# A nucleus search in a graph kernel: one full vector evaluation fewer and one aimed point more in step one

## Chip, cores and metric
The kernel runs on one core of a Trainium2 chip. The metric is the device time of one execution in microseconds, all float32. Engines are named as in the profile: PE (TensorE matmul), PEld (its weight loads), DVE (VectorE), ACT (ScalarE), POOL (GpSimd) and SP (SyncE, which issues the DMAs).

## What is computed
Four graph layers run over x (3327 rows of 256) and a sparse weighted 3327 x 3327 adjacency. The third layer is where the change sits. For each of its two steps every row of a dense attention matrix is cut to its nucleus, the largest entries that together hold 90% of the row:

```
n, D_ATTN, STEPS, P_NUC = 3327, 64, 2, 0.9
def _adj_from_feats(Xa, W1, W2, W3):
    logits = (Xa @ W1) @ W2 @ (Xa @ W3).T
    idx  = argsort(-logits, axis=1)
    csum = cumsum(softmax(sorted logits), axis=1)
    k_i  = sum(csum < P_NUC, axis=1) + 1
    keep the k_i largest of each row; return softmax(kept logits)
for s in range(STEPS):
    A  = _adj_from_feats(Xa, W1, W2, W3)
    Xf = Rf @ Xf;  Xb = Rb @ Xb;  Xa = A @ Xa
    Z  = Z + Xf @ U1[s] + Xb @ U2[s] + Xa @ U3[s]
Y = X + Z, then a layer norm, scaled and shifted
```

## The kernel before
The 3327 rows are padded to 26 tiles of 128 rows (NT = 26). Layers 0 and 1, layer 3 and the two attention steps are written as software pipelines. The attention part is one loop of `rounds`. In each round one tile is at each stage, and each engine runs its own written-out order. Steps one and two follow each other in the same loop: tiles 0 to 25 are step one, tiles 26 to 51 step two, with LAG = 5 rounds between them.

In a round, PE computes the scores of a tile L in four pieces (L910), the transposes of the finished tile T (L895), the product of its probabilities with the values (L882), the neighbour sums for another tile (L922) and small dense products (L929, L954, L958). ACT copies each of these out of PSUM: L1070 the scores into `E`, L1066 the transposes into `PT`, and others. PE can't go on to the next piece before ACT has copied. ACT also takes the exponential of tile F (L1075) and runs the passes of the aimed search (L1027). Every such pass reads the full tile of 128 x 3327.

The sorted nucleus isn't computed by sorting. A threshold for each row is searched in three parts:

- POOL makes a first guess of the threshold from the row's mean and sum (`guess`, L1204 to L1236).
- ACT evaluates an aimed point: a pass with `Relu` sums what lies above it (m = 0), a pass with `Sign` counts it (m = 1). `PASSES` is 2 for each point and `POINTS` is 2. POOL then corrects the threshold from the two sums (`update(t, j)`, L1238 to L1276), with a Newton-like step for the first point and a secant-like one for the second. Each point narrows a bracket `ends2`. The corrections work on columns of 128 x 1 to 128 x 4 elements, and `then` makes POOL wait for each group before it issues the next.
- DVE evaluates the threshold exactly (`find`, L1367 on) `EVALS` times: 3 in step one and 4 in step two. Each evaluation is one SCALAR_TENSOR_TENSOR over 128 x 3327 (L1399) with short instructions around it. Then L1406 collects what lies below the upper end, and a loop takes the eight largest remaining entries with MAX8 (L1420) and MATCH_REPLACE8 (L1430). The loop runs again if a row of the tile still needs more. L1446 writes the kept probabilities.

DVE's order in a round is the row maximum of tile F (L1361) and then `find` of tile S. The tiles stand two rounds apart: F = shown(i - 1), R = shown(i - 2), S = shown(i - 3), T = shown(i - 4).

POOL's order in a step-one round is: guess(F), update(R, 1), the two adds of the neighbour sums of tile G (L1328, L1332), update(F, 0). The second point of a tile is thus corrected one round after its first. In step two the adds and layer norm pieces of further tiles stand around these (L1296 to L1347).

ACT's order: piece 0 ends with the exponential of F and then sums(R, 1, 0). Piece 1 ends with sums(R, 1, 1), piece 2 with sums(F, 0, 0). Piece 3 has sums(F, 0, 1) right after the copy of the last scores. `aimed[j]` tells ACT that point j is there, `summed[j]` tells POOL that a pass is done, `bracketed` tells DVE that the aimed search has ended.

Of the kernel before, what the change touches and what calls it, by code (L numbers as in the profile page):

```python
# [13 lines left out]
P = 128  # L14
# [18 lines left out]
UNDER = 1.0 - 2.0 ** -22  # L33
# [41 lines left out]
def build(nc, n_nodes, xin, adjT, W0T, b0, W1g, A1T, A2, A3, UA, UB, UC, gamma, beta, tin, Wg3, out):  # L75
# [13 lines left out]
    with ctx:  # L89
# [551 lines left out]
        with ExitStack() as att:  # L641
# [11 lines left out]
            sign = ab("sign", [P, 2, POINTS])  # L653
            negp = ab("negp", [P, 2, POINTS])
            known = ab("known", [P, 8])
            outset = ab("outset", [P, 2, 2, 2])
            ga = ab("ga", [P, 2, 20])
            up = ab("up", [P, 2, 24])
            cand = ab("cand", [P, 2, 3])
# [49 lines left out]
            kept = len(spread)  # L709
            turned = lambda i: sum(first(sent_at(k)) or first(post_at(k)) for k in range(i))  # L710
# [3 lines left out]
            with phase_semaphores(nc, "att_") as s:  # L714
# [30 lines left out]
                summed = [s(f"summed{j}") for j in range(POINTS)]  # L745
                aimed = [s(f"aimed{j}") for j in range(POINTS)]
                step_done, bracketed = s("aim_step"), s("bracketed")

                with nc.Block() as block:
# [264 lines left out]
                    def _(act):  # L1014
                        go = nc.scalar.activation

                        def sums(t, j, m):
                            if m == 0:
                                act.wait_ge(aimed[j], t + 1)
                                if j > 0:  # L1020
                                    act.wait_ge(summed[j - 1], PASSES[j - 1] * (t + 1))
                                elif t >= 1:
                                    act.wait_ge(summed[1], 2 * t)
                            else:
                                act.wait_ge(summed[j], 2 * t + 1)
                            func, acc_ = ((ACT.Relu, over), (ACT.Sign, sign))[m]
                            go(junk[:, 0:N], E[:, t % DEPTH, 0:N], func, bias=negp[:, t % 2, j:j + 1], scale=1.0,  # L1027
                               accum_out=acc_[:, t % 2, j:j + 1]).then_inc(summed[j], 1)

                        for i in range(rounds):  # L1030
# [11 lines left out]
                            for k in range(SLOTS):  # L1042
# [38 lines left out]
                                if k == 0 and R is not None:  # L1081
                                    sums(R, 1, 0)
# [84 lines left out]
                    def _(pool):  # L1167
# [3 lines left out]
                        KNOWN = (1.0 / ROOT, -1.0, 0.5, float(np.e), AIM[0], STEER[0], AIM[1], STEER[1])  # L1171
# [21 lines left out]
                        def offer(t, j):  # L1193
                            then(ts(negp[:, t % 2, j:j + 1], cand[:, t % 2, 0:1], -UNDER, None, ALU.mult))
                            pool.sem_inc(aimed[j], 1)

                        def prepare(t):
                            q, step = t % 2, t // NT
                            p = cand[:, q, 0:1]
                            then(ts(up[:, q, 0:2], known[:, 4 + 2 * step:6 + 2 * step], p, ga[:, q, 12:13], ALU.mult, ALU.add),  # L1200
                                 ts(up[:, q, 3:4], p, p, RIDGE[step] ** 2, ALU.mult, ALU.mult))
                            then(tt(up[:, q, 4:5], up[:, q, 3:4], ga[:, q, 11:12], ALU.mult))

                        def guess(t):  # L1204
# [5 lines left out]
                            p = cand[:, q, 0:1]  # L1210
                            pool.wait_ge(exp_done, t + 1)
                            if t >= DEPTH:
# [14 lines left out]
                            offer(t, 0)  # L1227
# [7 lines left out]
                                 ts(ga_(11), ga_(15), ga_(9), 1.0 / DENSITY, ALU.mult, ALU.mult))  # L1235
                            prepare(t)  # L1236

                        def update(t, j):  # L1238
                            q, d, step = t % 2, t % DEPTH, t // NT
                            up_ = lambda a: up[:, q, a:a + 1]  # L1240
                            restart()
                            p, gap_p, slip = (cand[:, q, a:a + 1] for a in range(3))
                            slope = ga[:, q, 11:12]
                            ends = ends2[:, d]
                            lo, hi = ends2[:, d, 0, 0:1], ends2[:, d, 1, 0:1]
                            tgt, point = trial2[:, d, GOAL:GOAL + 1], trial2[:, d, POINT:POINT + 1]
                            count, mass_ = up_(5 + j), up_(8 + j)
                            pool.wait_ge(summed[j], PASSES[j] * (t + 1))
                            then(ts(count, sign[:, q, j:j + 1], 0.5, N / 2, ALU.mult, ALU.add))
                            then(ts(mass_, count, p, over[:, q, j:j + 1], ALU.mult, ALU.add))  # L1250
                            then(ts(cand[:, q, 1:3], up[:, q, 0:2], mass_, None, ALU.add),
                                 ts(took[:, 1:2], mass_, tgt, None, ALU.is_ge))
                            if j > 0:
                                then(tt(up_(16), mass_, up_(7 + j), ALU.subtract))
                                then(ts(up_(17), up_(16), up_(16), up_(3), ALU.mult, ALU.add),
                                     tt(up_(18), up_(16), up_(20), ALU.mult))
                                then(tt(up_(19), up_(17), minus, ALU.pow),
                                     tt(up_(18), up_(4), up_(18), ALU.subtract))
                                then(tt(slope, up_(18), up_(19), ALU.mult))
                            then(tt(up_(21), slip, slope, ALU.mult),  # L1260
                                 ts(took[:, 0:3:2], took[:, 1:2].to_broadcast([P, 2]), -1.0, 1.0, ALU.mult, ALU.add))
                            wide = lambda ap: ap.unsqueeze(2).to_broadcast([P, 2, 2])
                            then(ts(up_(20), up_(21), STRIDE, -STRIDE, ALU.min, ALU.max),
                                 tt(parts[:, 0], ends, wide(took[:, 0:2]), ALU.mult),
                                 tt(parts[:, 1], cand[:, q, 0:2].unsqueeze(1).to_broadcast([P, 2, 2]),
                                    wide(took[:, 1:3]), ALU.mult))
                            then(tt(up_(22), e_, up_(20), ALU.pow),
                                 tt(ends, parts[:, 0], parts[:, 1], ALU.add))
                            then(tt(up_(23), up_(22), p, ALU.mult))
                            if j < POINTS - 1:  # L1270
                                then(ts(p, up_(23), hi, lo, ALU.min, ALU.max))
                                offer(t, j + 1)
                                prepare(t)
                            else:
                                then(ts(point, up_(23), hi, lo, ALU.min, ALU.max))
                                pool.sem_inc(bracketed, 1)  # L1276

# [10 lines left out]
                        for i in range(rounds):  # L1288
# [37 lines left out]
                            if first(G):  # L1326
# [166 lines left out]
```

## Time and profile before

| | us |
|---|---|
| median of 3 runs | 3486.06 (3485.86 to 3487.74) |
| the profiled execution | 3488.64 |
| its span in the profile | 3486.8 |
| PE, DVE, POOL, ACT busy | 3144.3, 2454.0, 2146.4, 1599.1 |

The span is from the first to the last instruction. Row maxima of step one (L1361) start from 818.56 to 1759.36 us, those of step two from 1899.43 to 3090.95 us. The page's first part gives the busy shares, 90% for PE, 70% for DVE, 62% for POOL and 46% for ACT. They are means over all layers. The chain that ended last is 6% of the span on PE's L294 in the last layer, and it says nothing about the attention stage.

### The profile page before, as it was taken

How to read it: one execution, taken by the hardware profiler on the slowest of the kernel's cores; microseconds unless marked ns; L12 is line 12 of the kernel's file. 1: busy time of each engine (PE TensorE's matmuls, PEld its weight loads, DVE VectorE, ACT ScalarE, POOL GpSimd, SP SyncE). 2: the span in 40 equal slices, each digit the busy share in tenths (PEclk: the TensorE clock that was granted, in tenths of full speed). 3: DMA queues.
4: the chain of work that ended last, by engine and by line, in shares of the span. 5: the costliest groups of instructions: out<-in, count | busy, mean ns of one | idle time of the engine just before them, and what ended most of it. 6: DMA issues, size and time to landing. Idle time of an engine off the chain costs nothing. (4 is left out here: it accounts for less than half of the span.)

```text
span 3486.8 us, 42119 instructions
## 1 busy us (share of the span) xinstructions
PE 3144.3 (90%) x13212; PEld 2272.6 (65%) x13212; DVE 2454.0 (70%) x3451; ACT 1599.1 (46%) x2357; POOL 2146.4 (62%) x4214
## 2 busy tenths in 40 slices
PE   4999989998699999999976698988899999996899
PEld 3788878885477777777754254544566566664788
DVE  6983410002998889888884799999978999998000
ACT  2211321225566666666653455555555655552200
POOL 1212421124788888888880677877988788886211
PEclk9999999998899999999988899999999999998899
DMA  6643444443122122112211111211222222223254
GB/s 246 223 162 132 130 147 163 163 142 86 44 58 58 58 58 66 54 59 63 65 33 62 47 52 52 62 44 56 57 81 76 73 84 82 74 83 102 91 201 172
DMA packets 140702, 327.59 MB, mean 94 GB/s; under 512 B 15456, under 2 KB 93664, under 8 KB 129248
## 3 DMA queue, kind: packets, MB, share of 16 engines
q1 hardware_dynamic: 140512, 325.30, 29.3%
q8 instruction: 90, 1.47, 0.2%
q14 instruction: 100, 0.82, 0.1%
HBM read 286.70 MB, written 38.54 MB: 93 GB/s over the span
## 5 line engine op out<-in xcount | busy, mean ns | idle before, releaser
L1027 ACT ACTIVATE junk<-E,negp 128x3327 uint8<-128x3327 f32 x208 | 637.3, 3064 | 142.4 <-issue 107.8
L1399 DVE SCALAR_TENSOR_TENSOR U<-E,trial 128x3327 f32<-128x3327 f32 x182 | 678.5, 3728 | 0.0
L922 PE MATMUL bank<-big,adj 128*128 128x512 f32 x1352 | 609.9, 602 | 8.7 <-ACT t L1053 8.7
L922 PEld LDWEIGHTS bank<-big,adj 128*128 128x128 f32 x1352 | 252.9, 192 | 329.2 <-issue 328.1
L294 PE MATMUL bank<-big,E 128*128 128x256 f32 x1664 | 366.2, 381 | 2.4 <-PEq L58 1.7
L882 PE MATMUL bank<-Hc,PT 128*128 128x256 f32 x1248 | 305.1, 396 | 69.2 <-ACT PT L1066 69.2
L294 PEld LDWEIGHTS bank<-big,E 128*128 128x128 f32 x1664 | 315.9, 191 | 49.3 <-issue 6.6
L882 PE MATMUL bank<-Hc,adj 128*128 128x256 f32 x1456 | 335.4, 382 | 10.7 <-ACT adj L1066 10.7
L1361 DVE TENSOR_REDUCE nmax<-E 128x1 f32<-128x3327 f32 x52 | 188.0, 3615 | 207.4 <-ACT E L1070 207.4
L882 PEld LDWEIGHTS bank<-Hc,PT 128*128 128x128 f32 x1248 | 245.9, 199 | 129.9 <-ACT PT L1066 79.7
L882 PEld LDWEIGHTS bank<-Hc,adj 128*128 128x128 f32 x1456 | 277.8, 191 | 72.9 <-issue 23.0
L922 PE MATMUL bank<-Hc,adj 128*128 128x256 f32 x1352 | 314.2, 383 | 1.0 <-ACT bias L1047 1.0
L922 PEld LDWEIGHTS bank<-Hc,adj 128*128 128x128 f32 x1352 | 253.6, 191 | 78.7 <-issue 48.6
L895 PE MATMUL tr<-ident,E 128*128 128x128 f32 x1352 | 192.4, 283 | 119.9 <-DVE E L1446 119.8
L1420 DVE MAX8 top<-U 128x8 f32<-128x3327 f32 x74 | 268.4, 3627 | 21.8 <-DVE mass L1408 11.9
L352 POOL TENSOR_TENSOR xn<-xt,t 128x256 f32<-128x256 f32 x52 | 37.7, 724 | 386.9 <-ACT t L325 205.8
L1430 DVE MATCH_REPLACE8 U<-mark,U 128x3336 f32<-128x3336 f32 x74 | 267.7, 3618 | 0.0
L895 PEld LDWEIGHTS tr<-ident,E 128*128 128x128 f32 x1352 | 168.4, 147 | 145.7 <-DVE E L1446 125.5
L910 PE MATMUL lg<-K,qt 64*128 64x384 f32 (+1 forms) x832 | 215.4, 596 | 33.1 <-ACT E L1070 25.2
L366 DVE TENSOR_TENSOR t<-bank,big 128x256 f32<-128x256 f32 x26 | 11.0, 425 | 286.9 <-PE bank L294 286.9
L1066 ACT ACTIVATE adj<-tr 128x1024 f32<-128x1024 f32 x104 | 95.4, 918 | 251.1 <-PE tr L895 251.1
L1070 ACT ACTIVATE E<-lg 128x1024 f32<-128x1024 f32 x208 | 179.4, 863 | 54.1 <-PE lg L910 48.7
(248 smaller groups left out, 5937.2 us busy)
## 6 DMA issues: line engine op xcount, KB each, us to landing
adj<-adjT SPq DMA_DIRECT2D x131, 448.0 KB, 3.4
E<-adjT SPq DMA_DIRECT2D x32, 1664.0 KB, 6.9
adj<-adjT SPq DMA_DIRECT2D x104, 384.0 KB, 3.4
adj<-adjT SPq DMA_DIRECT2D x20, 1664.0 KB, 7.0
E<-adjT SPq DMA_DIRECT2D x26, 1216.0 KB, 5.7
xt<-xin SPq DMA_DIRECT2D x52, 128.0 KB, 5.7
x_d<-xn SPq DMA_DIRECT2D x52, 128.0 KB, 1.7
xt<-x_d SPq DMA_DIRECT2D x52, 128.0 KB, 5.2
```

The costliest lines, as they stand in the source:

```text
L294: last = nc.tensor.matmul(acc[par][:, 0:D], bufs[par][:, j], rhs[:, j], start=(j == j0), stop=(j == NT - 1))
L882: last = mm(axp[:, 0:D], PT[k % 2][:, h, i * P:(i + 1) * P], Hc[:, j], start=(k == 0 and h == 0 and i == 0), stop=(k == SLOTS - 1 and h == ...
L895: last = nc.tensor.transpose(tr[:, h, i * P:(i + 1) * P], E[:, t % DEPTH, c0:c0 + P], ident[:])
L910: last = mm(lg[:, h, 0:w], qt[rows, t % 2], K2[rows, c0:c0 + w], start=True, stop=True)
L922: last = mm(agg[:, 0:w], adj[:, SPAN * (k % 2) + j - AGG[k]], rhs[:, j], start=(j == 0), stop=False)
L1027: go(junk[:, 0:N], E[:, t % DEPTH, 0:N], func, bias=negp[:, t % 2, j:j + 1], scale=1.0, accum_out=acc_[:, t % 2, j:j + 1]).then_inc(summed ...
L1066: go(PT[k % 2][:, :, 0:w], tr[:, :, 0:w], ACT.Copy).then_inc(pt_copied, 1)
L1070: go(halves(E[:, L % DEPTH])[:, :, c0:c0 + w], lg[:, :, 0:w], ACT.Copy, accum_out=musum[:, L % 2, k:k + 1]).then_inc(lg_copied, 1)
L1361: V_.tensor_reduce(nmax[:, t % DEPTH:t % DEPTH + 1], E[:, t % DEPTH, 0:N], axis=AX_X, op=ALU.max, negate=True).then_inc(max_ready, 1)
L1399: V_.scalar_tensor_tensor(out=U[:, 0:N], in0=e, scalar=point, in1=e, op0=ALU.is_ge, op1=ALU.mult, accum_out=found))
L1420: rthen(V_.memset(U[:, N:NPAD], 0.0), V_.max(top8[:], U[:, 0:N]))
L1430: V_.match_replace(U[:], mark[:], U[:], MARKED).then_inc(rnd, 1)
```

## The change
Step one gets three aimed points instead of two (`POINTS = (3, 2)`), and two exact evaluations instead of three. Step two keeps two points and four evaluations. The third point has a `Sign` pass only. The constants of the search change too. `summed` becomes one semaphore that counts ACT's passes in ACT's order.

ACT runs sums(R, 1, 0) at the end of piece 1, just ahead of sums(R, 1, 1), and no longer in piece 0. In step one sums(R, 2, 1) stands in piece 2, ahead of sums(F, 0, 0). POOL gets update(R, 2) in step one between the adds of tile G and update(F, 0).

`update` is rewritten. The first point goes from the counted pass to the next `negp` in five dependent steps, the second in eight. The new `negp` is the old one times the correction factor, without the clamp to the bracket. The bracket and the preparation of the next point come after `aimed` has been raised.

```diff
-EVALS = (3, 4)
+EVALS = (2, 4)
-PASSES = (2, 2)
-POINTS = 2
-SHIFT = (1.4, 0.0)
-STEER = (2.0, 4.0)
-AIM = (3.0, 4.0)
-KEEP_END = (0.8, 0.75)
+POINTS = (3, 2)
+SHIFT = (1.2, 0.0)
+AIM = (2.0, 4.0)
+KEEP_END = (0.8, 0.85)
-UNDER = 1.0 - 2.0 ** -22
+UNDER = 1.0 - 2.0 ** -20
...
                                 if k == 0 and R is not None:
-                                    sums(R, 1, 0)
...
                                     if R is not None:
+                                        sums(R, 1, 0)
                                         sums(R, 1, 1)
...
+                                    if R is not None and POINTS[R // NT] > 2:
+                                        sums(R, 2, 1)
                                     if F is not None:
                                         sums(F, 0, 0)
...
                         def prepare(t):
-                            p = cand[:, q, 0:1]
-                            then(ts(up[:, q, 0:2], known[:, 4 + 2 * step:6 + 2 * step], p, ga[:, q, 12:13], ALU.mult, ALU.add),
-                                 ts(up[:, q, 3:4], p, p, RIDGE[step] ** 2, ALU.mult, ALU.mult))
-                            then(tt(up[:, q, 4:5], up[:, q, 3:4], ga[:, q, 11:12], ALU.mult))
+                            up_ = lambda a: up[:, q, a:a + 1]
+                            p = up_(24)
+                            then(ts(up_(2), p, N / 2 + AIM[step], ga[:, q, 12:13], ALU.mult, ALU.add),
+                                 ts(up[:, q, 0:2], known[:, 4 + 2 * step:6 + 2 * step], p, None, ALU.mult),
+                                 ts(up_(3), p, p, RIDGE[step] ** 2, ALU.mult, ALU.mult))
+                            then(tt(up_(4), up_(3), ga[:, q, 11:12], ALU.mult))
...
                         def guess(t):
+                            then(ts(cand[:, q, 0:1], p, 1.0, None, ALU.mult))
                             prepare(t)
...
                         def update(t, j):
+                            if j < 2:
+                                pool.wait_ge(summed, nth[t, j, 0])
+                                then(tt(up_(5), over[:, q, j:j + 1], up_(2), ALU.add))
+                            pool.wait_ge(summed, nth[t, j, 1])
+                            if j < 2:
+                                then(ts(slip, signs, up_(0), up_(5), ALU.mult, ALU.add))
+                            else:
+                                then(ts(slip, signs, up_(16), up_(17), ALU.mult, ALU.add))
+                            if j == 0:
+                                then(ts(up_(13), slip, slope, STRIDE, ALU.mult, ALU.min))
+                            else:
+                                then(tt(up_(7), slip, up_(6), ALU.subtract))
+                                then(ts(up_(8), up_(7), up_(7), up_(3), ALU.mult, ALU.add),
+                                     ts(up_(9), up_(7), up_(10), up_(4), ALU.mult, ALU.add))
+                                then(tt(up_(11), up_(8), minus, ALU.pow),
+                                     tt(up_(12), up_(9), slip, ALU.mult))
+                                then(ts(up_(13), up_(12), up_(11), STRIDE, ALU.mult, ALU.min))
+                            then(ts(up_(14), up_(13), -STRIDE, None, ALU.max))
+                            then(tt(up_(15), e_, up_(14), ALU.pow))
+                            if not last:
+                                then(tt(negp[:, q, j + 1:j + 2], negp[:, q, j:j + 1], up_(15), ALU.mult))
+                                pool.sem_inc(aimed[j + 1], 1)
+                            if j < 2:
+                                then(ts(took[:, 1:2], slip, up_(1), None, ALU.is_ge),
+                                     tt(up_(21), up_(15), p, ALU.mult))
+                            else:
+                                then(ts(up_(18), signs, up_(19), up_(20), ALU.mult, ALU.add),
+                                     tt(up_(21), up_(15), p, ALU.mult))
+                                then(ts(took[:, 1:2], up_(18), 0.0, None, ALU.is_ge))
+                            then(ts(took[:, 0:3:2], took[:, 1:2].to_broadcast([P, 2]), -1.0, 1.0, ALU.mult, ALU.add))
+                            then(tt(parts[:, 0], ends, wide(took[:, 0:2]), ALU.mult),
+                                 tt(parts[:, 1], cand[:, q].unsqueeze(1).to_broadcast([P, 2, 2]),
...
+                            then(tt(ends, parts[:, 0], parts[:, 1], ALU.add))
+                            if last:
+                                then(ts(point, up_(21), hi, lo, ALU.min, ALU.max))
                                 pool.sem_inc(bracketed, 1)
+                                return
+                            if j == 1:
+                                then(tt(up_(22), slip, up_(1), ALU.subtract),
+                                     tt(up_(23), signs, up_(0), ALU.mult),
+                                     ts(up_(19), p, 0.5, None, ALU.mult),
+                                     tt(up_(25), up_(21), p, ALU.add),
+                                     tt(up_(26), up_(21), p, ALU.subtract),
+                                     tt(slope, up_(9), up_(11), ALU.mult))
+                                then(tt(up_(20), up_(22), up_(23), ALU.subtract),
+                                     ts(up_(16), up_(25), 0.25, None, ALU.mult),
+                                     ts(up_(27), up_(26), AIM[step], slip, ALU.mult, ALU.add))
+                                then(tt(up_(28), signs, up_(16), ALU.mult))
+                                then(tt(up_(17), up_(27), up_(28), ALU.subtract))
+                            then(ts(cand[:, q, 0:1], up_(21), hi, lo, ALU.min, ALU.max),
+                                 ts(p, up_(21), 1.0, None, ALU.mult),
+                                 ts(up_(6), slip, 1.0, None, ALU.mult),
+                                 ts(up_(10), up_(14), -1.0, None, ALU.mult))
+                            prepare(t)
...
+                            if R is not None and POINTS[R // NT] > 2:
+                                update(R, 2)
                             if F is not None:
                                 update(F, 0)
```

`tt` is a TENSOR_TENSOR on POOL, `ts` a TENSOR_SCALAR; instructions inside one `then` don't wait for each other.

## Rows read from the trace of the kernel before

**Rows 1.** Stretches: us, busy (x) of PE, PEld, DVE, ACT, POOL, granted clock, DMA.
```profile
859.27:1016.88 157.61, 128.49 (x565) 92.81 (x564) 151.32 (x218) 98.76 (x113) 126.00 (x240) 0.91 0.19 53
1016.88:1759.36 742.48, 706.12 (x3266) 530.48 (x3266) 657.94 (x944) 494.63 (x590) 645.49 (x1192) 0.98 0.21 59
1999.12:3038.88 1039.76, 974.11 (x3495) 582.92 (x3496) 976.24 (x1448) 577.16 (x780) 852.19 (x1579) 0.97 0.23 65
```

**Rows 2.** Row maxima and exact evaluations of step one (ns min/median/max, starts).
```profile
L1361 DVE TENSOR_REDUCE nmax<-E x24: 3604/3619/3620, 859.3 to 1759.4; 128x1 f32<-128x3327 f32 x24
...
L1399 DVE SCALAR_TENSOR_TENSOR U<-E,trial x57: 3671/3678/4225, 1022.4 to 1733.4; 128x3327 f32<-128x3327 f32 x57
```

**Rows 3.** Waits, step one (1016.88 to 1759.36), each engine: us, times, longest.
```profile
POOL up L1249 <- ACT junk L1027: 4.5, 5, 1.5
...
ACT junk L1027 <- issue: 87.7, 14, 9.0
...
DVE nmax L1361 <- ACT E L1070: 58.1, 16, 5.9
```

**Rows 4.** Timeline, POOL and DVE side by side (start, duration).
```profile
1222.73 3.67 DVE L1399 SCALAR_TENSOR_TENSOR U<-E,trial 128x3327 f32<-128x3327 f32 x1
1222.79 3.66 POOL L1263 TENSOR_SCALAR up<-up 128x1 f32<-128x1 f32 x1
```

**Rows 5.** Timeline of POOL beside DVE's L1430 and just ahead of and beside L1361 (start, duration).
```profile
1240.95 0.55 POOL L1226 TENSOR_TENSOR cand<-known,ga 128x1 f32<-128x1 f32 x1
1241.59 0.23 POOL L1194 TENSOR_SCALAR negp<-cand 128x1 f32<-128x1 f32 x1
...
1249.19 0.34 POOL L1250 TENSOR_SCALAR up<-up,cand,over 128x1 f32<-128x1 f32 x1
1249.63 0.30 POOL L1251 TENSOR_SCALAR cand<-up 128x2 f32<-128x2 f32 x1
1249.91 0.29 POOL L1252 TENSOR_SCALAR took<-up,trial 128x1 f32<-128x1 f32 x1
1250.28 0.19 POOL L1254 TENSOR_TENSOR up<-up 128x1 f32<-128x1 f32 x1
...
1250.88 0.19 POOL L1256 TENSOR_TENSOR up<-up 128x1 f32<-128x1 f32 x1
1251.15 0.57 POOL L1257 TENSOR_TENSOR up<-up,known 128x1 f32<-128x1 f32 x1
...
1252.22 0.19 POOL L1260 TENSOR_TENSOR up<-cand,ga 128x1 f32<-128x1 f32 x1
1252.38 0.19 POOL L1261 TENSOR_SCALAR took<-took 128x2 f32<-128x2 f32 x1
```

**Rows 6.** Timeline of DVE, one round of step one.
```profile
1371.18 3.61 DVE L1361 TENSOR_REDUCE nmax<-E 128x1 f32<-128x3327 f32 x1
...
1380.20 3.68 DVE L1399 SCALAR_TENSOR_TENSOR U<-E,trial 128x3327 f32<-128x3327 f32 x1
1385.48 3.68 DVE L1399 SCALAR_TENSOR_TENSOR U<-E,trial 128x3327 f32<-128x3327 f32 x1
...
1406.05 3.61 DVE L1361 TENSOR_REDUCE nmax<-E 128x1 f32<-128x3327 f32 x1
```

**Rows 7.** MAX8 passes: all, then those up to 1870 us.
```profile
L1420 DVE MAX8 top<-U x74: 3626/3627/3629, 881.9 to 3212.9; 128x8 f32<-128x3327 f32 x74
...
L1420 DVE MAX8 top<-U x29: 3626/3627/3629, 881.9 to 1850.9; 128x8 f32<-128x3327 f32 x29
```

**Rows 8.** Waits of POOL and DVE, step two (1999.12 to 3038.88).
```profile
POOL stat L1314 <- ACT junk_x L1080: 40.5, 6, 13.4
POOL ga L1214 <- ACT E L1075: 23.0, 2, 17.3
POOL up L1249 <- ACT junk L1027: 19.5, 9, 4.1
...
DVE nmax L1361 <- ACT E L1070: 24.6, 4, 10.3
```

More of the change, by code:

```diff
@@ L652, in build @@
             over = ab("over", [P, 2, 2])
-            sign = ab("sign", [P, 2, POINTS])
-            negp = ab("negp", [P, 2, POINTS])
+            sign = ab("sign", [P, 2, 3])
+            negp = ab("negp", [P, 2, 3])
             known = ab("known", [P, 8])
             outset = ab("outset", [P, 2, 2, 2])
-            ga = ab("ga", [P, 2, 20])
-            up = ab("up", [P, 2, 24])
-            cand = ab("cand", [P, 2, 3])
+            ga = ab("ga", [P, 2, 16])
+            up = ab("up", [P, 2, 32])
+            cand = ab("cand", [P, 2, 2])
             took = ab("took", [P, 3])
@@ L709, in build @@
             kept = len(spread)
+            passes = []
+            for i in range(rounds):
+                R, F = aim_at(i), exp_at(i)
+                if R is not None:
+                    passes += [(R, 1, 0), (R, 1, 1)] + [(R, 2, 1)] * (POINTS[R // NT] - 2)
+                if F is not None:
+                    passes += [(F, 0, 0), (F, 0, 1)]
+            tiles_with = lambda t, j: sum(POINTS[x // NT] > j for x in range(t + 1))
+            nth = {which: i + 1 for i, which in enumerate(passes)}
             turned = lambda i: sum(first(sent_at(k)) or first(post_at(k)) for k in range(i))
@@ L744, in build @@
                 search, rnd = s("search_step"), s("round_step")
-                summed = [s(f"summed{j}") for j in range(POINTS)]
-                aimed = [s(f"aimed{j}") for j in range(POINTS)]
+                summed = s("summed")
+                aimed = [s(f"aimed{j}") for j in range(3)]
                 step_done, bracketed = s("aim_step"), s("bracketed")
@@ L1017, in sums @@
                         def sums(t, j, m):
[L1018 to L1025, printed above, removed]
+                            if m == 0 or j == 2:
+                                act.wait_ge(aimed[j], tiles_with(t, j))
+                            if nth[t, j, m] > 1:
+                                act.wait_ge(summed, nth[t, j, m] - 1)
                             func, acc_ = ((ACT.Relu, over), (ACT.Sign, sign))[m]
                             go(junk[:, 0:N], E[:, t % DEPTH, 0:N], func, bias=negp[:, t % 2, j:j + 1], scale=1.0,
-                               accum_out=acc_[:, t % 2, j:j + 1]).then_inc(summed[j], 1)
+                               accum_out=acc_[:, t % 2, j:j + 1]).then_inc(summed, 1)
                         for i in range(rounds):
@@ L1080, in _ @@
                                     go(junk_x[:], x3b[:, Y % 2], ACT.Copy, accum_out=stat3[:, Y % 2, 0:1]).then_inc(ln3_a, 1)
-                                if k == 0 and R is not None:
-                                    sums(R, 1, 0)
                                 if k == 1 and W is not None:
@@ L1170, in _ @@
                         ts = G_.tensor_scalar
-                        KNOWN = (1.0 / ROOT, -1.0, 0.5, float(np.e), AIM[0], STEER[0], AIM[1], STEER[1])
+                        KNOWN = (1.0 / ROOT, -1.0, 0.5, float(np.e), 0.5, AIM[0], 0.5, AIM[1])
                         values = [(known[:, i:i + 1], value) for i, value in enumerate(KNOWN)]
@@ L1209, in guess @@
                             tgt, below = (trial2[:, d, a:a + 1] for a in (GOAL, BELOW))
-                            p = cand[:, q, 0:1]
+                            p = up[:, q, 24:25]
                             pool.wait_ge(exp_done, t + 1)
@@ L1226, in guess @@
                             then(tt(p, e_, ga_(14), ALU.pow))
-                            offer(t, 0)
+                            then(ts(negp[:, q, 0:1], p, -UNDER, None, ALU.mult))
+                            pool.sem_inc(aimed[0], 1)
                             shape4 = lambda ap: ap.rearrange("p a b -> p (a b)")
@@ L1240, in update @@
                             up_ = lambda a: up[:, q, a:a + 1]
-                            restart()
-                            p, gap_p, slip = (cand[:, q, a:a + 1] for a in range(3))
-                            slope = ga[:, q, 11:12]
+                            last = j == POINTS[step] - 1
+                            p, slip, slope = up_(24), cand[:, q, 1:2], ga[:, q, 11:12]
                             ends = ends2[:, d]
                             lo, hi = ends2[:, d, 0, 0:1], ends2[:, d, 1, 0:1]
-                            tgt, point = trial2[:, d, GOAL:GOAL + 1], trial2[:, d, POINT:POINT + 1]
@@ L1247, in update @@
[L1247 to L1259, printed above, removed]
@@ L1260, in update @@
-                            then(tt(up_(21), slip, slope, ALU.mult),
-                                 ts(took[:, 0:3:2], took[:, 1:2].to_broadcast([P, 2]), -1.0, 1.0, ALU.mult, ALU.add))
-                            wide = lambda ap: ap.unsqueeze(2).to_broadcast([P, 2, 2])
-                            then(ts(up_(20), up_(21), STRIDE, -STRIDE, ALU.min, ALU.max),
-                                 tt(parts[:, 0], ends, wide(took[:, 0:2]), ALU.mult),
-                                 tt(parts[:, 1], cand[:, q, 0:2].unsqueeze(1).to_broadcast([P, 2, 2]),
-                                    wide(took[:, 1:3]), ALU.mult))
@@ L1267, in update @@
[L1267 to L1275, printed above, removed]
-                                pool.sem_inc(bracketed, 1)
+                            point = trial2[:, d, POINT:POINT + 1]
@@ new lines, in update @@
+                            signs = sign[:, q, j:j + 1]
+                            wide = lambda ap: ap.unsqueeze(2).to_broadcast([P, 2, 2])
+                            restart()
+                            if j < 2:
[6 more added lines that the diff above has]
+                                then(ts(slip, signs, up_(16), up_(17), ALU.mult, ALU.add))
```

3 lines of the change are left out of this document (removed).

## The prediction
> **What bounds the kernel now.** The page's parts on busy shares and on the last chain come first and are set aside. The shares mix four layers, and the chain that ended last lies wholly in the last layer. The change touches only the attention rounds, so I read the windows of those rounds. The reader should see that in step one PE is busy for 706.12 of 742.48 us, DVE for 657.94 and POOL for 645.49 [rows 1]. These 19 rounds take 39.08 us each. Over all of step one, 24 row maxima from 859.3 to 1759.4 us give 23 rounds of 39.1 us [rows 2].
>
> Three engines look full, so the waits must decide. DVE waited 58.1 us for a score copy of ACT, and ACT waited 87.7 us before its aimed passes, with "issue" as the releaser. That pass waits for `aimed`, which POOL raises. POOL itself waited 4.5 us for an ACT pass in 19 rounds, and for next to nothing else [rows 3]. So POOL is the engine that never waits in step one.
>
> Its 645.49 busy us leave 97 us of gaps. I don't count them as room: there are 1192 instructions, and 97/1192 = 0.08 us is the gap after a typical dependent one (0.19 us long, next start 0.27 us later) [rows 1, 5].
>
> POOL's time has a second part. A column operation that usually takes 0.19 us took 3.66 us when DVE's SCALAR_TENSOR_TENSOR started beside it, and ended with it [rows 4]. While DVE ran its row maximum, MAX8 or MATCH_REPLACE8, POOL kept its usual pace [rows 5]. I went through POOL's timeline of the 19 rounds, start to start, from L1249 at 1017 us on. Just 95 of the instructions lasted over 2 us. DVE has 95 such passes in that time, five a round (57 of L1399, 19 each of L1406 and L1446) [rows 2]. Beyond their usual spacing the 95 cost 319.7 us, 3.37 us each. The usual spacing of all 1192 instructions sums to 413.0 us, and 9.6 us is left over. 413.0 + 319.7 + 9.6 is the whole 742 us. A round is thus POOL's 21.7 us of open work, five blockings of 3.37 us, and 0.5 us of waiting.
>
> The Trainium skill ("SBUF — State Buffer", Who interferes with whom) says that a DVE operation with both inputs in SBUF blocks a GpSimd operation that reads SBUF, while a tensor_reduce never does. The trace agrees, with 3.66 us beside L1399 and 0.19 us beside L1361.
>
> Step two differs. Its 21 rounds take 49.5 us each. POOL waited 40.5, 23.0 and 19.5 us there, about 4 us a round [rows 8], and DVE is busy for 976.24 of 1039.76 us [rows 1].
>
> **The change, part by part, in step one.** DVE loses one evaluation, 5.28 us from one L1399 to the next [rows 6]. A round in which DVE never waits took 34.87 us [rows 6]; it would be 29.6. DVE doesn't set the round, so these 5.3 us are not a gain in themselves. What POOL gains is one blocking fewer, -3.37 us a round.
>
> ACT gains one pass, 3.1 us and its short read. It is busy 494.63/19 = 26.0 us a round [rows 1], so about 29.3. I cost it at nothing, covered by ACT's waits. The pass stands behind `aimed[2]`, and PE waits for the next copy behind it. From `aimed[2]` ACT needs three passes and two copies until `summed` is complete for update(F, 0), some 11.6 us. POOL meanwhile has the rest of update(R, 1), the adds and update(R, 2), some 6 + 1.8 + 5.8 = 13.6 us without blockings. Without that cover a round costs up to one pass more.
>
> POOL gains instructions. Prices, start to start [rows 5]: a dependent operation without a column as scalar 0.27 us, with one 0.37, with two 0.44, `pow` 0.64 (0.55 where a sibling follows), a sibling that needs no wait 0.16, with a column scalar 0.28.
> - update(R, 2) is new, 17 instructions: 8 x 0.27 + 0.37 + 3 x 0.44 + 0.64 + 0.55 + 2 x 0.28 + 0.16 = 5.8 us.
> - update(R, 1) goes from 19 to 36 instructions, as it now prepares a third point. By these prices 12 x 0.27 + 0.44 + 3 x 0.37 + 2 x 0.44 + 0.43 + 0.64 + 0.55 + 5 x 0.28 + 10 x 0.16 = 10.3 us, against 5.9. That is +4.4.
> - update(F, 0) goes from 17 to 20, 5.6 to 6.2 us: +0.6.
> - guess gets two more: +0.4.
>
> Together 39 instructions and +11.2 us. From below, 39 x 0.27 = 10.5; from above, 39 x 413.0/1192 = 13.5. I take 11.2, since siblings and `pow` are priced apart in it. That `aimed` comes after five or eight steps shortens ACT's wait, not POOL's list, and ACT is not the bound.
>
> A round of step one becomes 39.08 + 11.2 - 3.37 = 46.9 us, +7.8. It counts in 23 rounds between the maxima [rows 2] and in about two more at the start and in the drain (POOL's two longer updates of the last tile delay `bracketed`, and step two can't start before the last tile is through). 25 x 7.8 = 195 us.
>
> PE: with 37.2 us of work in 46.9 it is 79% busy. The granted clock was 0.98 at 95% busy and 0.91 at 82% [rows 1]; even at 0.91 its work would be 40 us, below 46.9. Cost nothing.
>
> **In step two** POOL gets the same guess and update(F, 0), +1.0 us, and the last update is as long as before (5.9). Its 4 us of waiting cover that in most rounds. Between 0 and 26 x 1.0 I take 8 us. The number of MAX8 loops depends on the constants. There were 74 passes for 52 tiles, 29 up to 1870 us, so 19 extra ones in step two and 3 in step one [rows 7]. A loop is 8.87 us of DVE. In step one DVE would have 46.9 - 29.6 = 17.3 us to spare, nearly two loops a tile, so a weaker bracket there costs nothing. In step two I assume no change, as points and evaluations are as many as before.
>
> Sum: 3488.64 + 195 + 8 = 3692 us for the profiled execution. It lies 2.6 us above the median of the runs shown, so 3689.
>
> **Rivals.**
> - *POOL waits for the third pass.* If ACT reaches it late, POOL waits a pass (3.3 us) in each round: 25 x 3.3 = 82 more, 3771. For it: ACT's order puts the pass behind four copies in piece 2. Against: 13.6 us of POOL work cover 11.6.
> - *More loops in step two.* One more in every second tile is 13 x 8.87 = 115, so 3804. For it: the new `negp` isn't clamped. Against: the step formula is the same in step two.
> - *POOL's gaps are room.* Taking its busy time at face value, 97/19 = 5.1 us a round are free, and only 11.2 - 3.4 - 5.1 = 2.7 would show: 25 x 2.7 = 68, so 3554 to 3620 with part of it. The Trainium skill ("Perfetto Trace Analysis", GPSIMD Engine Instruction) warns against reported spans of GpSimd and wants start-to-start spacing, which is how I counted.
> - *Faster.* The shorter DVE list wins, because rounds shrink to PE's 706.12/19 = 37.2 us: 25 x (39.08 - 37.2) = 47, so 3439. It decides as soon as POOL's added open work is below the 3.37 us of the lost blocking. Against it stand 39 instructions.
> - *No change.* Added work and lost blocking cancel; it needs the same few microseconds.
>
> **How the numbers follow.** Forecast 0.66, third pass 0.10, more loops 0.09, room in the gaps 0.07, faster 0.05, no change 0.03. Changes within 0.2% (7 us) are about what a measurement of this kernel can't tell from none. That makes faster 0.05, same 0.03, slower 0.92. The time is 3689. For the forecast alone the bounds are 24 x (10.5 - 3.4) = 170 and 27 x (13.5 - 3.4) = 273 us, with 0 to 26 in step two: 3656 to 3785. Some five loops fewer in step two would take 40 us off the lower end. With the third pass inside, the range is 3620 to 3780.
>
> **What the new profile would show.** Right: step-one maxima 46 to 48 us apart, some 102 POOL instructions a round, four of them blocked, POOL without waits for ACT, DVE waiting some 10 us a round before L1361, ACT waiting longer before L1027. The first step would be wrong if POOL waits in step one or if rounds are 37 to 39 us. The count of L1420 tells on the loops. The prediction fails if blockings are not one for one with the two-input passes, or if the new update is much shorter than priced.

## The result: 6.1% slower, and the profile after

The kernel after takes 3697.35 us (median of 4 runs, 3696.25 to 3699.24), against 3486.09 before. The ratio is 1.0606, with a 95% interval of 1.0587 to 1.0624. The forecast was 3689 us, with a range of 3620 to 3780.

The windows of step one (19 rounds from the row maximum at 1055.83 us) and of step two (21 rounds), columns as in [rows 1]:

```profile
1055.83:1946.17 890.34, 740.29 (x3269) 554.32 (x3269) 547.26 (x703) 552.39 (x628) 749.37 (x1920) 0.90 0.17 50
2210.10:3242.55 1032.45, 976.86 (x3483) 586.44 (x3484) 948.13 (x1414) 570.23 (x777) 885.95 (x1627) 0.97 0.23 66
```

A round of step one went from 39.08 to 890.34/19 = 46.86 us. All engines but POOL now have clear gaps in it: PE was busy for 95% of the time and is for 83%, DVE for 61% and ACT for 62%. POOL's own busy share is only 84%, so the shares alone would not name it. It has 101 instructions a round where there were 62.7. Step two hardly moved, from 49.5 to 49.2 us a round.

DVE's passes in the same 19 rounds (ns min/median/max, first and last start):

```profile
L1394 DVE TENSOR_REDUCE nmax<-E x20: 3618/3619/3620, 1055.8 to 1946.2; 128x1 f32<-128x3327 f32 x20
...
L1432 DVE SCALAR_TENSOR_TENSOR U<-E,trial x38: 3675/3679/3694, 1062.1 to 1910.9; 128x3327 f32<-128x3327 f32 x38
...
L1439 DVE SCALAR_TENSOR_TENSOR U<-E,ends x19: 3679/3679/3681, 1071.6 to 1915.1; 128x3327 f32<-128x3327 f32 x19
...
L1479 DVE SCALAR_TENSOR_TENSOR E<-U,E x19: 3603/3605/3607, 1084.4 to 1927.9; 128x3327 f32<-128x3327 f32 x19
```

That is four two-input passes a round, 76 in all. In POOL's timeline 76 instructions lasted over 2 us, one for each. Start to start they take 273.3 us; all the others take 617.0, and together they are the 890.3 us of the stretch. That leaves no room on POOL in any round. Three of the four in one round, in the timeline:

```profile
1249.68 3.68 DVE L1432 SCALAR_TENSOR_TENSOR U<-E,trial 128x3327 f32<-128x3327 f32 x1
1249.85 3.72 POOL L1258 TENSOR_SCALAR cand<-sign,up 128x1 f32<-128x1 f32 x1
...
1253.67 0.30 POOL L1262 TENSOR_SCALAR up<-cand,ga 128x1 f32<-128x1 f32 x1
1254.05 0.21 POOL L1270 TENSOR_SCALAR up<-up 128x1 f32<-128x1 f32 x1
1254.35 0.57 POOL L1271 TENSOR_TENSOR up<-known,up 128x1 f32<-128x1 f32 x1
1254.97 3.67 DVE L1432 SCALAR_TENSOR_TENSOR U<-E,trial 128x3327 f32<-128x3327 f32 x1
1255.00 3.70 POOL L1273 TENSOR_TENSOR negp<-negp,up 128x1 f32<-128x1 f32 x1
...
1259.17 3.68 DVE L1439 SCALAR_TENSOR_TENSOR U<-E,ends 128x3327 f32<-128x3327 f32 x1
...
1259.46 3.44 POOL L1282 TENSOR_SCALAR took<-took 128x2 f32<-128x2 f32 x1
...
1263.29 3.63 DVE L1453 MAX8 top<-U 128x8 f32<-128x3327 f32 x1 [0.24 <-DVE mass L1441]
1263.41 0.20 POOL L1286 TENSOR_TENSOR ends<-parts 128x4 f32<-128x4 f32 x1
```

The L1273 row writes the next `negp`, which ACT needs. It is the fifth step of the first point, and it stood still for 3.7 us. That is not so in every round: this second pass falls on L1273 in 5 of the 19 and on the next row, L1276, behind `aimed`, in 14. The first pass of a round falls on L1258, ahead of `aimed`, in 18 of the 19. Beside MAX8 POOL kept its pace (0.20 us).

The waits of the same stretch (us, times, longest), against [rows 3]:

```profile
POOL took L1276 <- POOL negp L1273: 8.3, 38, 0.5
...
ACT junk L1030 <- POOLq L1274: 235.0, 19, 13.1
...
DVE nmax L1394 <- ACT E L1073: 278.5, 19, 14.7
...
PE bank L889 <- ACT PT L1069: 150.0, 19, 8.7
```

The chain reads from the bottom up. PE waits for a copy of ACT, ACT waits 12 us a round for POOL's `aimed` (L1274), and DVE waits 14.7 us for ACT's score copy. POOL waits for nobody but itself. ACT's wait for `aimed` was 87.7 us in 19 rounds before ([rows 3], there with "issue" as the releaser) and is 235.0 now, though `aimed` is raised after fewer steps.

MAX8 passes, all and those of step one, against 74 and 29 in [rows 7]:

```profile
L1453 DVE MAX8 top<-U x69: 3626/3627/3628, 888.3 to 3423.4; 128x8 f32<-128x3327 f32 x69
...
L1453 DVE MAX8 top<-U x27: 3626/3627/3628, 888.3 to 2057.9; 128x8 f32<-128x3327 f32 x27
```

So two exact evaluations sufficed after three aimed points, and step two needed 42 passes where it had 45.

Where the 210.7 us of the span came from, by the first and last maxima of each step:

| | before | after | difference |
|---|---|---|---|
| start to first maximum | 818.6 | 818.2 | -0.4 |
| 25 rounds of step one | 940.8 | 1128.0 | +187.2 |
| drain between the steps | 140.1 | 162.5 | +22.4 |
| 25 rounds of step two | 1191.5 | 1184.2 | -7.3 |
| last maximum to the end | 395.9 | 404.6 | +8.8 |

### The profile page after: what moved, and what is told of

Read it like the earlier page. It is cut to its first block and busy times, and to the rows that moved or that the text cites. A ratio compares the mean times of both kernels' runs of the same rounds, so it can differ in the third digit from the quotient of the medians.

```text
span 3697.5 us, 43068 instructions
## 1 busy us (share of the span) xinstructions
PE 3200.8 (87%) x13212; PEld 2314.6 (63%) x13212; DVE 2269.8 (61%) x3084; ACT 1672.9 (45%) x2409; POOL 2346.8 (63%) x5306
## 5 line engine op out<-in xcount | busy, mean ns | idle before, releaser
L1030 ACT ACTIVATE junk<-E,negp 128x3327 uint8<-128x3327 f32 x234 | 717.4, 3066 | 341.2 <-POOLq L1274 324.0
L1432 DVE SCALAR_TENSOR_TENSOR U<-E,trial 128x3327 f32<-128x3327 f32 x156 | 579.2, 3713 | 0.0
L889 PE MATMUL bank<-Hc,PT 128*128 128x256 f32 x1248 | 341.4, 431 | 208.8 <-ACT PT L1069 208.8
L889 PEld LDWEIGHTS bank<-Hc,PT 128*128 128x128 f32 x1248 | 269.8, 219 | 281.3 <-ACT PT L1069 223.3
L889 PE MATMUL bank<-Hc,adj 128*128 128x256 f32 x1456 | 356.3, 399 | 40.5 <-ACT adj L1069 40.4
L889 PEld LDWEIGHTS bank<-Hc,adj 128*128 128x128 f32 x1456 | 290.8, 201 | 110.3 <-ACT adj L1069 51.7
L929 PE MATMUL bank<-Hc,adj 128*128 128x256 f32 x1352 | 318.2, 387 | 2.9 <-ACT bias L1050 2.9
L929 PEld LDWEIGHTS bank<-Hc,adj 128*128 128x128 f32 x1352 | 257.1, 194 | 81.7 <-issue 51.1
L1453 DVE MAX8 top<-U 128x8 f32<-128x3327 f32 x69 | 250.3, 3627 | 19.7 <-DVE mass L1441 11.5
L917 PE MATMUL lg<-K,qt 64*128 64x384 f32 (+1 forms) x832 | 215.0, 595 | 45.5 <-ACT E L1073 37.2
L1463 DVE MATCH_REPLACE8 U<-mark,U 128x3336 f32<-128x3336 f32 x69 | 249.6, 3618 | 0.0
L1439 DVE SCALAR_TENSOR_TENSOR U<-E,ends 128x3327 f32<-128x3327 f32 x52 | 197.9, 3806 | 2.2
L1479 DVE SCALAR_TENSOR_TENSOR E<-U,E 128x3327 f32<-128x3327 f32 x52 | 188.6, 3627 | 0.0
```

The source lines that it names most:

```text
L889: last = mm(axp[:, 0:D], PT[k % 2][:, h, i * P:(i + 1) * P], Hc[:, j], start=(k == 0 and h == 0 and i == 0), stop=(k == SLOTS - 1 and h == ...
L917: last = mm(lg[:, h, 0:w], qt[rows, t % 2], K2[rows, c0:c0 + w], start=True, stop=True)
L929: last = mm(agg[:, 0:w], adj[:, SPAN * (k % 2) + j - AGG[k]], rhs[:, j], start=(j == 0), stop=False)
L1432: V_.scalar_tensor_tensor(out=U[:, 0:N], in0=e, scalar=point, in1=e, op0=ALU.is_ge, op1=ALU.mult, accum_out=found))
L1439: V_.scalar_tensor_tensor(out=U[:, 0:N], in0=e, scalar=hi[:, 0:1], in1=e, op0=ALU.is_lt, op1=ALU.mult, accum_out=sc[:, 5:6]))
L1453: rthen(V_.memset(U[:, N:NPAD], 0.0), V_.max(top8[:], U[:, 0:N]))
```

## The experiments

The theory is that POOL alone sets the rounds of step one: its open work (39 column operations more) and one blocking for each two-input DVE pass. The rivals are that DVE's or ACT's list matters in itself, that POOL had room, and that the rounds follow ACT's wait for `aimed`. "Before" is 3485 to 3493 us beside all runs.

### The evaluation put back

```diff
-EVALS = (2, 4)
+EVALS = (3, 4)
```

> The kernel after with the third exact evaluation put back in step one. DVE would be at some 35 us in rounds of 46.9, so by DVE's own list nothing changes: 3697 us. POOL theory: five blockings in a round in place of four, 46.9 + 3.3 = 50.2 us, 25 x 3.3 = 83 us more, 3780 us.

Measured 3783.87 us (2 runs), span 3781.4, 86.5 us above the kernel after. The rounds take 50.5 us each by the maxima and five POOL instructions are blocked in each. DVE's list, some 35 us, is still far shorter than the round, so its length can't be the reason.

### A pass of either kind added

One more pass was put ahead of the evaluations of step one. Its result is written and not used.

```diff
+if step == 0:
+    then(V_.scalar_tensor_tensor(out=U[:, 0:N], in0=e, scalar=0.0, in1=e,
+                                 op0=ALU.is_ge, op1=ALU.mult, accum_out=sc[:, 7:8]))
```

> The kernel after with one more DVE pass in step one, with both inputs in SBUF, whose result isn't used. POOL theory: one more blocking a round, 25 x 3.3 = 83 us more, 3780 us. If DVE's length mattered in itself, it should cost the same as a tensor_reduce of the same length.

```diff
+if step == 0:
+    then(V_.tensor_reduce(sc[:, 7:8], e, axis=AX_X, op=ALU.max))
```

> The kernel after with one more DVE pass in step one, a tensor_reduce of 3.6 us over one input, whose result isn't used. POOL theory: no blocking and DVE has some 17 us to spare, so within 10 us of 3697. If DVE's list carried the round, or a pass of any kind blocked POOL: 83 us more, 3780.

With the two-input pass 3796.40 us, 99 above the kernel after; with the reduce 3699.14, 2 above (2 runs each). The passes are equally long. Row maxima, first those with the two-input pass:

```profile
L1394 DVE TENSOR_REDUCE nmax<-E x20: 3618/3619/3620, 1071.2 to 2031.8; 128x1 f32<-128x3327 f32 x20
```

And with the reduce:

```profile
L1394 DVE TENSOR_REDUCE nmax<-E x20: 3618/3619/3620, 1056.0 to 1945.3; 128x1 f32<-128x3327 f32 x20
```

Nineteen rounds in 960.6 us are 50.6 each, in 889.3 they are 46.8. The timeline of the run with the reduce shows POOL beside both kinds:

```profile
1296.07 3.62 DVE L1421 TENSOR_REDUCE sc<-E 128x1 f32<-128x3327 f32 x1 [2.42 <-POOLq L1289]
...
1297.27 0.21 POOL L1270 TENSOR_SCALAR up<-up 128x1 f32<-128x1 f32 x1
1297.57 0.57 POOL L1271 TENSOR_TENSOR up<-known,up 128x1 f32<-128x1 f32 x1
1298.21 0.19 POOL L1273 TENSOR_TENSOR negp<-negp,up 128x1 f32<-128x1 f32 x1
...
1299.92 3.68 DVE L1434 SCALAR_TENSOR_TENSOR U<-E,trial 128x3327 f32<-128x3327 f32 x1
1300.18 3.62 POOL L1303 TENSOR_SCALAR cand<-up,ends 128x1 f32<-128x1 f32 x1
```

Under the reduce POOL started eleven operations. This pair of runs settles that the kind of pass counts, not its time on DVE. The round grew by 3.7 us, against the 3.3 expected: the fifth blocking cost 3.4 beyond its usual spacing, and the other four cost a little more than in the kernel after. The maxima of step one took 85.0 us more and the drain 10.8 (173.3 us against 162.5), while the 83 us expected were to hold both.

### Ten column operations more on POOL

```diff
 update(R, 2)
+for _ in range(5):
+    then(ts(pad[:, 1:2], pad[:, 0:1], 0.5, None, ALU.mult))
+    then(ts(pad[:, 0:1], pad[:, 1:2], 2.0, None, ALU.mult))
```

> The kernel after with ten dependent column operations more on POOL behind the third correction in step one; their results aren't used. POOL theory: 10 x 0.28 = 2.8 us a round, 25 x 2.8 = 70 us more, 3767 us. If POOL's gaps or waits were room: 3697 us.

Measured 3774.56 us (2 runs), 77 above. The maxima:

```profile
L1399 DVE TENSOR_REDUCE nmax<-E x20: 3618/3619/3621, 1068.5 to 2014.4; 128x1 f32<-128x3327 f32 x20
```

945.9/19 = 49.8 us a round, 2.9 more for ten operations. The added work shows one to one in the round.

### ACT's third pass made twice

```diff
 if R is not None and POINTS[R // NT] > 2:
+    act.wait_ge(aimed[2], tiles_with(R, 2))
+    act.wait_ge(summed, nth[R, 2, 1] - 1)
+    go(junk[:, 0:N], E[:, R % DEPTH, 0:N], ACT.Sign, bias=negp[:, R % 2, 2:3], scale=1.0,
+       accum_out=pad[:, R % 2:R % 2 + 1]).then_inc(twice, 1)
+    act.wait_ge(twice, R + 1)
     sums(R, 2, 1)
```

> The kernel after with ACT's pass for the third point made twice in step one; the first of the two isn't used. The theory has some 13.6 us of POOL work over 11.6 us of ACT work, so a second pass of 3.3 us is 1 to 2 us too long for the cover: 0 to 35 us more, 3697 to 3732 us. If ACT's passes carried the round: 25 x 3.3 = 82 us more, 3780 us.

Measured 3712.32 us (2 runs), 15 above the kernel after; the rounds take 47.5 us. Of a pass of 3.3 us, 0.7 showed. It doesn't show as a wait of POOL, whose longest wait for a pass of ACT in these rounds is short:

```profile
POOL up L1262 <- ACT junk L1032: 4.6, 18, 0.3
```

The kernel after has a gap of the same size at this place (0.26 us), so POOL lost next to nothing by waiting. Most of the 0.7 us lies in the four blockings: 13.7 us a round beyond usual spacing, against 13.2. They fall on other operations of POOL than before; why each then costs 0.1 us more wasn't tried. So the third pass itself was free, and a second one was covered too.

### Two points and three evaluations in the new code

```diff
-EVALS = (2, 4)
-POINTS = (3, 2)
+EVALS = (3, 4)
+POINTS = (2, 2)
```

> The kernel after with two points and three exact evaluations in step one, so the rewritten corrections and the new constants without the third point. POOL theory: guess +0.4 and the first correction +0.6 us against the kernel before, the second as long as before, five blockings: 39.1 + 1.0 = 40.1 us a round, 25 us more in step one; step two as in the kernel after, near 0. 3505 to 3520 us. If the five and eight step order shortens the round (ACT's waits carried part of it): 3486 or less.

Measured 3570.24 us, ratio 1.0237 (1.0220 to 1.0254), 50 us above the upper end of what was expected. The rounds themselves are as expected: 40.1 to 40.3 us from the fifth maximum to the eighteenth. Then some are longer, by the timeline of DVE:

```profile
1418.41 3.61 DVE L1394 TENSOR_REDUCE nmax<-E 128x1 f32<-128x3327 f32 x1
1458.63 3.61 DVE L1394 TENSOR_REDUCE nmax<-E 128x1 f32<-128x3327 f32 x1
1525.78 3.61 DVE L1394 TENSOR_REDUCE nmax<-E 128x1 f32<-128x3327 f32 x1
```

The first interval is 40.2 us, the second 67.2. Three tiles of step one needed 4, 3 and 6 MAX8 passes, and their rounds took 67.2, 56.9 and 85.0 us. Step one has 36 passes, where the kernel before had 29. The rounds right behind the three took 34.8 us, less than the usual 40.2, and made up for a part. The correction therefore costs its +1.0 us a round, and the surplus over the expectation comes from three tiles in which the bracket stayed wide. Which constant or which step of the rewritten correction widens it wasn't tried.

### Two evaluations in the kernel before

```diff
-EVALS = (3, 4)
+EVALS = (2, 4)
```

> The kernel before with two exact evaluations in step one and nothing else. POOL theory: a round of step one loses one blocking, 39.1 - 3.4 = 35.7 us on POOL, which is below PE's 37.2 us of work; rounds become 37.2 to 38 us and the time falls by 25 x 1 to 1.9, to 3440 to 3465 us. If DVE's blockings didn't matter for POOL: rounds stay at 39.1 and the time at 3486. If the bracket gets too wide: MAX8 passes of step one rise well above 29, and a tile with two loops puts DVE at 38.5 us.

Measured 3739.05 us, ratio 1.0720 (1.0702 to 1.0738), 274 us above the upper end. I had put the loops down as a side case, and they are the result:

```profile
L1420 DVE MAX8 top<-U x74: 3626/3627/3628, 876.2 to 2026.3; 128x8 f32<-128x3327 f32 x74
```

Up to its last step-one tile the run has 79 passes, 74 of them by 2026.3 us, against 29. In the stretch from 1055.83 to 1780 us PE waited 152.5 us for DVE's L1446, in ten waits, and POOL 212.3 us for ACT's exponential. With 3 passes a tile DVE sets the round, 50.5 us on the mean. So two points don't suffice for two evaluations with the constants and the correction of the kernel before. Three points with two evaluations (27 passes) are about as sharp as two with three (29). That the third point does this, and not the new constants, wasn't run by itself: two points and two evaluations in the new code are missing. Against the constants stands the run above, where the new code needed 36 passes with two points and three evaluations.

### The adds of tile G moved to DVE

```diff
 # POOL, step one: the two adds of tile G, L1328 and L1332, left out
 # DVE, one round later, ahead of the row maximum
+H = sent_at(i - 1) if i >= 1 else None
+if first(H):
+    dve.wait_ge(zt_copied, H + 1)
+    V_.tensor_tensor(t0[:, 0], t0[:, 0], t0[:, 1], ALU.add).then_inc(t_ready, 1)
+    dve.wait_ge(t_ready, H + 1)
+    if H >= 2:
+        dve.wait_ge(zg_out[H % 2], 16 * (H // 2))
+    V_.tensor_tensor(xz[:, H % 2], t0[:, 0], Hc[:, H], ALU.add).then_inc(z_step, 1)
+    dve.wait_ge(z_step, H + 1)
+    dve.sem_inc(zg_done, 1)
 if F is not None:
     row_max(F)
```

SP stores the tile one round later too.

> The kernel before with the two 128x256 adds of tile G in step one made by DVE, ahead of its row maximum one round later, instead of by POOL. POOL theory: 39.1 - 1.8 = 37.3 us a round on POOL, PE's work is 37.2: some 1.5 to 1.8 us less in 25 rounds, 3441 to 3455 us. If PE or DVE already held the round, 3486 us; if the adds collide with POOL or make ACT wait, above 3486.

Measured 3455.54 us, ratio 0.9911 (0.9894 to 0.9927). It is 32 us below the kernel before, run beside it: a small gain of 0.9%, with an interval that lies clear of 1. Nineteen rounds take 37.2 us each. Most single ones are shorter, by DVE's timeline:

```profile
1054.44 0.42 DVE L1447 TENSOR_TENSOR t<-t 128x256 f32<-128x256 f32 x1
1054.89 0.42 DVE L1451 TENSOR_TENSOR adj<-t,Hc 128x256 f32<-128x256 f32 x1
1055.47 3.62 DVE L1353 TENSOR_REDUCE nmax<-E 128x1 f32<-128x3327 f32 x1 [0.16 <-DVE adj L1451]
1090.30 0.42 DVE L1447 TENSOR_TENSOR t<-t 128x256 f32<-128x256 f32 x1
1090.75 0.43 DVE L1451 TENSOR_TENSOR adj<-t,Hc 128x256 f32<-128x256 f32 x1
1091.34 3.62 DVE L1353 TENSOR_REDUCE nmax<-E 128x1 f32<-128x3327 f32 x1 [0.16 <-DVE adj L1451]
```

35.9 us from one maximum to the next, with no wait on DVE. That is its 34.9 us [rows 6] and 1.0 for the two adds. In rounds of 37.1 us DVE waits for POOL. POOL and DVE now share the bound. PE may be at it too: in this round of 35.87 us it is busy throughout, at a granted clock of 1.00.

```profile
1055.47:1091.34 35.87, 35.87 (x170) 27.11 (x169) 34.52 (x52) 25.74 (x30) 31.42 (x57) 1.00 0.23 65
```

### The same move in the kernel after

> The kernel after with the two 128x256 adds of tile G in step one moved from POOL to DVE, as in adds_on_dve. POOL holds all of a round's 46.9 us here and PE is far away with 37.2, so the whole 1.8 us must show in each round: 45.0 to 45.1 us, 25 x 1.8 = 45 us less, 3652 us. If two short DVE adds block POOL as well, 0.5 to 1 us of it is lost: 3665 to 3680 us. If POOL doesn't hold the round: 3697.

Measured 3660.03 us, ratio 1.0492 (1.0475 to 1.0510), 37 us below the kernel after, with rounds mostly of 45.4 us. POOL lost 1.8 us of work a round and 1.4 of them showed. DVE's two adds have two inputs in SBUF as well and are 0.84 us together. The trace shows a part of the rest beside them, in the two operations of POOL that follow its blocked L1237:

```profile
1082.07 0.27 POOL L1238 TENSOR_SCALAR trial<-trial 128x1 f32<-128x1 f32 x1
1082.45 0.41 POOL L1239 TENSOR_SCALAR ga<-ga 128x1 f32<-128x1 f32 x1
```

The same two take 0.22 and 0.26 us in the kernel after. That is 0.2 us a round. The other 0.2 to 0.3 lies in operations that the adds don't touch, and its cause is open.

### The new KEEP_END on top

```diff
-KEEP_END = (0.8, 0.75)
+KEEP_END = (0.8, 0.85)
```

> adds_on_dve with the new KEEP_END of step two (0.85 in place of 0.75), the only part of the change that can have taken MAX8 passes out of step two without POOL work. If it is the cause of the 42 passes where there were 45: 3 x 8.87 = 27 us less of DVE, of which DVE's and POOL's nearly equal lists let 5 to 20 us show: 3435 to 3450 us. If the rewritten correction is the cause, or UNDER, step two keeps 45 passes and the time is 3455 us.

Measured 3449.13 us, ratio 0.9889 (0.9873 to 0.9906), the best of all. The 25 rounds of step two took 1175.9 us in place of 1188.2 with 43 MAX8 passes in place of 45. Tile by tile, KEEP_END takes one pass from each of the three tiles (the 2nd, 19th and 22nd of step two) that also lose one by the whole change, and gives one more to the 25th, which the whole change does not. So it accounts for all three passes that went; what spares the 25th tile in the kernel after is open. The added pass falls behind the last maximum, where this run takes 402.5 us against 397.0. The gain of 6.4 us against adds_on_dve lies within the expected 5 to 20, but the intervals of the two ratios overlap; it is the count of passes and the 12.3 us between the maxima that tell the two apart.

## Why the prediction was right

**POOL holds the round.** Right. POOL's timeline of the 19 rounds has no gap that is left over, and five runs carry it: adding operations, adding a two-input pass (two runs), adding another kind of pass and taking operations away. The new `aimed` after five or eight steps made nothing faster, since POOL's whole list sets the round. ACT's wait grew, and DVE's before its row maximum became 14.7 us a round, where some 10 were forecast.

**The size of the list.** 39 instructions were forecast, and 101 less 62.7 are 38.3. Their open work was put at +11.2 us. After, the unblocked POOL instructions of a round take 32.48 us, and the four blocked would take 1.2 by their usual spacing, so 33.7 in all. Before it was 21.7 and 0.5 of waiting, 22.2. Unrounded, that is +11.4.

**One blocking fewer.** One for one with the two-input passes held exactly, 95 for 95 and 76 for 76. Its worth was a little off: 14.4 - 1.2 = 13.2 us for four, against 16.8 for five, so -3.6 in place of -3.37. The two misses of a quarter microsecond cancel, hence the round of 46.86 against the forecast 46.9. The agreement is closer than the terms, and that is luck.

**Number of rounds.** 25 rounds at 7.8 us were to cover the maxima and the drain, 195 us. The 23 intervals from the third maximum on gave 178.4, against 179.4 forecast. The ends were taken at some 16 us and gave 31: the second interval of the filling took 29.6 us in place of 20.8, and the drain 22.4 more. 8.9 us of the drain are a MAX8 loop. The last tile of step one took two passes where it took one in the kernel before:

```profile
2035.27 0.21 DVE L1430 TENSOR_SCALAR sc<-trial 128x1 f32<-128x1 f32 x1 [10.08 <-POOLq L1289]
...
2049.06 3.63 DVE L1453 MAX8 top<-U 128x8 f32<-128x3327 f32 x1 [0.24 <-DVE mass L1441]
...
2057.92 3.63 DVE L1453 MAX8 top<-U 128x8 f32<-128x3327 f32 x1 [0.46 <-DVE U L1463]
...
2066.61 3.60 DVE L1479 SCALAR_TENSOR_TENSOR E<-U,E 128x3327 f32<-128x3327 f32 x1
```

The prediction put a weaker bracket in step one at nothing, as DVE has 17.3 us to spare in a round. In the drain there is no next round to spare them in: DVE had waited 10 us for POOL's `bracketed`, and step two can't start before the last tile is through. Two of the experiments bear it out. With the added two-input pass the last tile still took two MAX8 passes, and the drain is 10.8 us longer than in the kernel after. With the third evaluation put back it took one, and the drain is only 1.6 us longer.

**Step two.** Forecast at +8; measured -7.3 between the maxima and +8.8 after the last one, so +1.5. I had assumed the MAX8 passes unchanged, and three went. At 8.87 us each they are 27 us of DVE, of which only a part showed. POOL's waits for ACT fell from about 4 to 2 us a round, as its longer list predicted. The 8.8 us after the last maximum are POOL's longer list again. DVE waits for `bracketed` ahead of both of the last two tiles:

```profile
3343.44 0.21 DVE L1430 TENSOR_SCALAR sc<-trial 128x1 f32<-128x1 f32 x1 [8.65 <-POOLq L1289]
...
3387.40 0.21 DVE L1430 TENSOR_SCALAR sc<-trial 128x1 f32<-128x1 f32 x1 [6.93 <-POOLq L1289]
```

Before, it waited 5.80 us ahead of the last and not at all ahead of the one before it. The last probabilities are begun 139.2 us after the last maximum, where it was 130.6.

**Why the total came so close.** Step one with its ends was 14 us too low and step two 6.5 too high, so the 8 us between 3689 and 3697 are in part two misses that cancel.

**PE.** It was costed at nothing with 37.2 us of work a round. It was busy for 740.29/19 = 39.0 us at a granted clock of 0.90, still well below 46.9.

**The rivals.** Waiting for the third pass is excluded by POOL's waits, which name no pass of ACT, and by the doubled pass, which cost 15 us, not 82. That POOL's gaps are room was excluded by the ten added operations. The faster case needed added work below 3.37 us. "More loops" was priced for step two, and it was the greater danger in step one: the kernel before with two evaluations took 79 passes there. Two more a tile, 2 x 8.87 = 17.7 us, would have used up the 17 us that DVE has to spare, had the third point been weak.

**A number of mine that was no floor.** I took 37.2 us of PE busy time as PE's work in a round. With the adds on DVE single rounds took 35.9 with the usual 170 matmuls in them. The granted clock was 1.00 in such a round and 0.98 in the 19; 37.2 x 0.98 = 36.4 us, an estimate, so it can be a part of the difference. The 34.9 us of [rows 6] prove less: PE had only 155 matmuls in that window.

## What to carry to other kernels

Count blockings, not busy shares: where GpSimd never waits, as here, its round is its own start-to-start work and one stop for each two-input VectorE pass over SBUF. Where GpSimd waits for others, some passes fall into its waits (in the kernel before with two evaluations 53 of 76 stopped it). A pass removed from VectorE is then worth the stop (3.3 to 3.7 us a round here), and it must not be bought with more than that many microseconds of GpSimd work (a dozen dependent column operations). When the engine that raises a semaphore was full, raising it earlier in its list bought nothing here; moving two adds off it did help. A cleanup loop that is covered in the steady rounds can show in full in the last one. Before an iteration of a search is dropped, ask what the cleanup loop behind it costs for the worst row of a tile.

## What the runs showed of the hardware

- A one-input tensor_reduce of 3.62 us on VectorE left GpSimd at its usual 0.19 to 0.57 us an operation. A two-input SCALAR_TENSOR_TENSOR of 3.68 us stopped it in every one of the 171 cases counted. The difference was 97 us on the whole kernel (3796.40 against 3699.14).
- PE showed 95% busy at a granted clock of 0.98 in rounds of 39.1 us. With two adds moved from POOL to DVE and the same matmuls (3257 in 19 rounds against 3266) the rounds took 37.2 us, single ones 35.9. A busy share near one didn't mean that PE held the round.
- In step one of the kernel after PE was 83% busy, and the granted clock was 0.90 against 0.98 before, while PE waited 150 us in 19 rounds for copies, so the clock didn't set the round.
